# Edge counts of a graph network built in groups of 18 targets instead of 25, with packed group numbers and counts stored in pieces

## What is computed

```python
h = relu(layernorm(x)); x = x + relu(segment_sum((h @ W0)[src] * w[:, None], dst))          # layer 0
h = relu(layernorm(x)); deg, norm ...; x = x + relu(segment_sum(norm * (h @ W1.T + b)[row], col))  # layer 1, with self loops
h = relu(layernorm(x)); a = h + segment_sum(h[src], dst); x = x + relu(a @ G1 + g1) @ G2 + g2  # layer 2
h = relu(layernorm(x)); x = x + concat of 8 heads of softmax-weighted segment_sum(Wx[src], dst) # layer 3
```

## Time and profile before

| | |
|---|---|
| median of 3 executions | 2926.83 us (2922.68 to 2935.74) |
| the profiled execution's own time | 2952.38 us |
| its span, first to last instruction | 2951.1 us |
| mean granted TensorE clock | 0.933 |
| PE busy | 2508.8 us, 85% |
| DVE busy | 1854.8 us, 63% |
| ACT busy | 568.5 us, 19% |
| POOL busy | 872.3 us, 30% |
| build loop, first to last matmul | 801.6 to 1153.7 us |

### The profile page before, as it was taken

How to read it: one execution, slowest core, us unless ns; L and a number is a source line. 1 busy time by engine, 2 the same in 40 slices (tenths; PEclk the granted TensorE clock), 3 DMA queues, 4 the chain that set the end, 5 groups by cost and what they waited for, 6 DMA issues and landing times.

```text
span 2951.1 us, 39280 instructions
## 1 busy us (share of the span) xinstructions
PE 2508.8 (85%) x10397; PEld 1450.1 (49%) x10397; DVE 1854.8 (63%) x4953; ACT 568.5 (19%) x946; POOL 872.3 (30%) x900
## 2 busy tenths in 40 slices
PE   7888988877887777999989999997898588888777
PEld 5534443433444444666555555664787433333332
DVE  7765667586588885657333443334786387776666
ACT  4533310000055553000000000001555100000000
POOL 0366666666400000000000000000002466666665
PEclk9899999898888888999999999998999699999999
DMA  6686655666422112334711121112644466676665
GB/s 164 178 241 175 181 166 167 172 168 179 117 75 86 54 54 65 94 110 112 200 43 57 57 57 54 53 32 61 152 120 138 125 193 202 204 230 189 192 189 167
DMA packets 152926, 389.06 MB, mean 132 GB/s; under 512 B 40735, under 2 KB 42136, under 8 KB 152737
## 3 DMA queue, kind: packets, MB, share of 16 engines
q0 software_dynamic: 71040, 232.25, 27.6%
q1 hardware_dynamic: 81014, 153.03, 18.4%
q10 hardware_dynamic: 683, 1.28, 0.2%
HBM read 333.73 MB, written 52.72 MB: 131 GB/s over the span
## 4 chain that ended last, share of the span: by engine, by line
PE 53%; DVE 23%; issue 10%; DMA 7%; another core or an unknown queue 3%; POOL 2%; ACT 1%; SPq 1%; ACTq 0%; DVEq 0%
PE banks L1841 17%; PE banks L1979 15%; PE banks L1807 7%; DVE spare L1031 4%; PE banks L2156 4%; DVE spare L1030 3%; DMA ring<-edge_counts 3%; PE banks L1971 3%; DMA ring<-table,src_t 2%; POOL ring L2313 2%; DVE sel L1104 2%; PE banks L1796 1%; DVE ring L1583 1%; DVE rstd L884 1%
## 5 line engine op out<-in xcount | busy, mean ns | idle before, releaser
L1841 PE MATMUL banks<-ring,sel 128*125 128x512 f32 x1682 | 891.4, 658 | 160.5 <-issue 116.1
L1841 PEld LDWEIGHTS banks<-ring,sel 128*125 128x125 f32 x1682 | 287.0, 199 | 476.7 <-issue 473.4
L2258 POOL DMA_INDIRECT ring<-table,src_t x440 | 436.8, 993 | 250.5 <-issue 107.7
L2292 POOL DMA_INDIRECT x<-table,src_t x25 | 25.1, 1005 | 1493.1 <-DMA x<-src_digits 1478.4
L2313 POOL DMA_INDIRECT ring<-table,src_t x401 | 386.5, 964 | 227.9 <-PE banks L1845 98.4
L1979 PE MATMUL banks<-acc,ring 125*125 125x512 f16 x1900 | 437.9, 381 | 7.0 <-issue 7.0
L1971 PE MATMUL banks<-spare 128*125 128x325 f16 x1080 | 276.0, 370 | 73.2 <-DVE spare L1031 24.2
L1979 PEld LDWEIGHTS banks<-acc,ring 125*125 125x125 f16 x1900 | 256.9, 137 | 160.4 <-issue 27.2
L1583 DVE TENSOR_TENSOR ring<-ring,banks 128x512 f32<-128x512 f32 x388 | 255.7, 682 | 122.3 <-DMA ring<-table,src_t 99.2
L1971 PEld LDWEIGHTS banks<-spare 128*125 128x125 f16 x1080 | 152.2, 147 | 197.2 <-issue 194.7
L1031 DVE TENSOR_SCALAR spare<-node_scores,flags 128x650 f16<-128x650 f16 x540 | 207.7, 385 | 0.0
(11 more groups left out here) (408 smaller groups left out, 2970.9 us busy)
## 6 DMA issues: line engine op xcount, KB each, us to landing
ring<-edge_counts SPq DMA_DIRECT2D x38, 683.6 KB
edge_counts<-big SPq DMA_DIRECT2D x25, 683.6 KB
ring<-table,src_t POOLq DMA_INDIRECT x841
sel<-edge_counts SPq DMA_DIRECT2D x12, 683.6 KB
acc<-dst_places SPq DMA_DIRECT2D x28, 256.0 KB
x<-dst_places SPq DMA_DIRECT2D x27, 256.0 KB
acc<-src_digits SPq DMA_DIRECT2D x28, 224.0 KB
x<-src_digits SPq DMA_DIRECT2D x27, 224.0 KB
```

The source lines that it names most:

```text
L1841: last = P.matmul(to, sel[:, n % SELS, :], rows, start=False, stop=True, skip_group_check=True)
L2258: G.indirect_dma_start(out=ring[:, i % RING, :], out_offset=None, in_=table[0][:, :], in_offset=bass.IndirectOffsetOnAxis(ap=src_t[:, i:i ...
```

## The change

A group becomes 18 targets (the last one of a tile 17), 7 groups to a tile, 175 in all, so `BSTEPS` is 590. The key is 25 x 18 = 450 wide and fits one PSUM bank of 512: a step has one matmul instead of two, and four banks take turns (`MADE`) instead of two pairs. The group numbers of three steps are packed into one 32-bit word by DVE (`GROUP_PACK`, `GROUP_BITS`), so 20 registers last for 60 steps; PE shifts and masks. ACT loads the ends of four tiles' groups (28 registers) at once. The one-hot of the low number is made for five steps (`LB`) by one `tensor_tensor`, with a semaphore of its own (`low_ok`); the ring grows to 10. A tile of counts is stored, and the first four are loaded, in eight pieces of up to 16 rows, stores spread over the time of the next tile. ACT's border counts in layer 0 go from 124 to 174, and the tables of the groups grow with them.

```diff
-    GT = 5
-    GW_N = TN // GT
+    GT = 7
+    GW_N = -(-TN // GT)
+    GW_LAST = TN - (GT - 1) * GW_N
-    KEY_W = 2 * HALF_W
-    HOTS = 7
+    KEY_W = TILES * GW_N
+    HOTS = 10
+    GROUP_PACK, GROUP_BITS, GROUP_WORDS = 3, 8, 20
+    END_TILES = 4
+    MADE = 4
-    COUNTS_FIRST, COUNTS_EACH = 24, 10
+    COUNTS_FIRST, COUNTS_EACH = 34, 14
+    PIECES = -(-TN // 16)
...
-            return banks[:, 2 * n:2 * n + 2, 0:HALF_W]
+            return banks[:, n % MADE, 0:KEY_W]
...
+                if b == BRB - 1:
+                    own.mark(V.memset(group_row[:, BSTEPS:LISTED], float(GROUPS)))
+                    V.wait_ge(v_own, own.n)
+                    number = group_row.rearrange("p (w n) -> p w n", n=GROUP_PACK)
+                    for n in range(GROUP_PACK - 1, 0, -1):
+                        high = number[:, :, n] if n == GROUP_PACK - 1 else group_sum
+                        own.mark(V.tensor_scalar(out=group_sum, in0=high, scalar1=float(1 << GROUP_BITS), scalar2=None, op0=ALU.mult))
+                        V.wait_ge(v_own, own.n)
+                        own.mark(V.tensor_tensor(group_sum, group_sum, number[:, :, n - 1], ALU.add))
+                        V.wait_ge(v_own, own.n)
+                    own.mark(V.tensor_copy(group_words, group_sum))
+                    V.wait_ge(v_own, own.n)
...
                 if j >= HOTS:
                     V.wait_ge(built, j - HOTS + 1)
-                V.tensor_scalar(out=low_hot[j % HOTS], in0=low_names, scalar1=low_t[:, j:j + 1], scalar2=None, op0=ALU.is_equal).then_inc(hot_ok, 1)
+                if j % LB == 0:
+                    if j >= HOTS:
+                        V.wait_ge(built, j - HOTS + LB)
+                    V.tensor_tensor(low_room[:, j % HOTS:j % HOTS + LB, :], low_names[:, None, :].to_broadcast([128, LB, TN]),
+                                    low_t[:, j:j + LB, None].to_broadcast([128, LB, TN]), ALU.is_equal).then_inc(low_ok, 1)
                 V.tensor_scalar(out=key_hot[j % HOTS], in0=key_names, scalar1=key_t[:, j:j + 1], scalar2=None, op0=ALU.is_equal).then_inc(hot_ok, 1)
...
                     if q == 0:
-                        A.reg_load(end_regs[0:GT], group_end[0:1, n:n + GT])
+                        if t % END_TILES == 0:
+                            tiles_left = min(END_TILES, TILES - t) * GT
+                            A.reg_load(group_regs[0:tiles_left], group_end[0:1, n:n + tiles_left])
...
             for j in range(BSTEPS):
-                if j % LOADED_TILES == 0:
-                    P.reg_load(tile_regs, group_row[0:1, j:j + LOADED_TILES])
+                if j % GROUP_STEPS == 0:
+                    P.reg_load(tile_regs[0:GROUP_WORDS], group_words[0:1, j // GROUP_PACK:j // GROUP_PACK + GROUP_WORDS])
...
-                v = nc.s_assert_within(P.snap(tile_regs[j % LOADED_TILES]) & 127, 1, GROUPS,
+                word, at = P.snap(tile_regs[j // GROUP_PACK % GROUP_WORDS]), j % GROUP_PACK * GROUP_BITS
+                v = nc.s_assert_within((word >> at if at else word) & 255, 1, GROUPS,
-                P.wait_ge(hot_ok, 2 * (j + 1))
+                P.wait_ge(hot_ok, j + 1)
+                if j % LB == 0:
+                    P.wait_ge(low_ok, j // LB + 1)
                 P.wait_ge(room, v)
-                for h in range(2):
-                    to = banks[0:TN, bass.ds((v & 1) * 2 + h, 1), 0:HALF_W].rearrange("p a d -> p (a d)")
-                    last = P.matmul(to, low_hot[j % HOTS], key_hot[j % HOTS][:, h * HALF_W:(h + 1) * HALF_W],
-                                    start=False, stop=True, skip_group_check=True)
-                last.then_inc(built, 1)
+                to = banks[0:TN, bass.ds(v & (MADE - 1), 1), 0:KEY_W].rearrange("p a d -> p (a d)")
+                P.matmul(to, low_hot[j % HOTS], key_hot[j % HOTS], start=False, stop=True, skip_group_check=True).then_inc(built, 1)
...
-            def store_counts(t):
-                S.wait_ge(taken, GT * (t + 1))
+            def store_counts(t, piece):
+                S.wait_ge(taken, min(GROUPS, GT * (t + 1) + piece * GT // PIECES))
-                S.dma_start(counts_dram[t * TN:t * TN + TOP, :], rows[0:TOP]).then_inc(stored[(COUNTS_N + t) % 3], 16)
-                S.dma_start(counts_dram[t * TN + TOP:(t + 1) * TN, :], rows[TOP:TN]).then_inc(stored[(COUNTS_N + t) % 3], 16)
+                p0, p1 = 16 * piece, min(TN, 16 * piece + 16)
+                S.dma_start(counts_dram[t * TN + p0:t * TN + p1, :], rows[p0:p1]).then_inc(stored[(COUNTS_N + t) % 3], 16)
```

More of the change, by code:

```diff
@@ L251, in build @@
         acc16 = flat_acc.bitcast(F16).rearrange("p (t c) -> p t c", c=2 * D)
[L253 removed]
+        made16 = [big[:, n * MAKE_W:(n + 1) * MAKE_W].bitcast(F16)[:, 0:TILES * TN].rearrange("p (s r) -> p s r", r=TN) for n in range(MAKES)]
         slot16 = [flat_ring[:, n * SLOT_W:(n + 1) * SLOT_W].bitcast(F16)[:, 0:TILES * TN] for n in range(SLOTS - 1)]
@@ L258, in counts_at @@
             return slot16[n % SLOTS][0:TN, s * TN:(s + 1) * TN]
+        LB = 5
+        assert HOTS % LB == 0 and BSTEPS % LB == 0
         HOT_W = KEY_W // 2 + (TN + 1) // 2
-        key_hot = [flat_spare[:, n * HOT_W:n * HOT_W + KEY_W // 2].bitcast(F16) for n in range(HOTS)]
-        low_hot = [flat_spare[:, n * HOT_W + KEY_W // 2:(n + 1) * HOT_W].bitcast(F16)[:, 0:TN] for n in range(HOTS)]
+        key_hot = [flat_spare[:, n * KEY_W // 2:(n + 1) * KEY_W // 2].bitcast(F16) for n in range(HOTS)]
+        low_room = flat_spare[:, HOTS * KEY_W // 2:HOTS * KEY_W // 2 + HOTS * TN // 2].bitcast(F16).rearrange("p (n i) -> p n i", i=TN)
+        low_hot = [low_room[:, n, :] for n in range(HOTS)]
         assert HOTS * HOT_W <= 6 * D
@@ L489, in build @@
         keys_ok, keys_turned = signal("keys_ok"), signal("keys_turned")
-        hot_ok, built, room, taken = signal("hot_ok"), signal("built"), signal("room"), signal("taken")
+        hot_ok, low_ok, built, room, taken = signal("hot_ok"), signal("low_ok"), signal("built"), signal("room"), signal("taken")
         slot_in = [signal(f"slot_in{n}") for n in range(SLOTS)]
@@ L549, in place_value @@
         def place_value(k):
-            return 32 * len(range(k % NB, 2 * TILES, SLOTS)) + 16 * (k // NB + 1)
+            return slot_value(2 * TILES - SLOTS + (k - 2 * TILES) % SLOTS) + 16 * (k // NB + 1)
         TABLE_N, COUNTS_N, H2_N, LAST_N = (n * TILES for n in range(4))
         def wait_stored(engine, n):
-            engine.wait_ge(stored[n % 3], 32 * (n // 3 + 1))
+            engine.wait_ge(stored[n % 3], sum(16 * PIECES if COUNTS_N <= m < H2_N else 32 for m in range(n % 3, n + 1, 3)))
         def pair_step(n):
@@ L648, in vector_program @@
             own.mark(V.tensor_copy(gstep_f[:, :], gstep_i[:, :]))
-            V.tensor_scalar(out=group_bias, in0=node_iota[:, 0:GROUPS - 1], scalar1=-float(GW_N), scalar2=0.5 - GW_N, op0=ALU.mult,
-                            op1=ALU.add).then_inc(consts, 1)
+            starts = group_start.rearrange("p (t q) -> p t q", q=GT)
+            own.mark(V.tensor_scalar(out=starts, in0=node_iota[:, 0:TILES, None].to_broadcast([128, TILES, GT]), scalar1=-float(TN), scalar2=0.5,
+                                     op0=ALU.mult, op1=ALU.add))
+            V.wait_ge(v_own, own.n)
+            V.scalar_tensor_tensor(out=starts, in0=node_iota[:, None, 0:GT].to_broadcast([128, TILES, GT]), scalar=-float(GW_N), in1=starts,
+                                   op0=ALU.mult, op1=ALU.add).then_inc(consts, 1)
             def step_tables():
@@ L1648, in count_groups @@
                                  accum_out=group_counts[:, g:g + 1]).then_inc(group_counted, 1)
+            group_regs = [A.alloc_register(f"group_end{n}") for n in range(END_TILES * GT)]
             def take_groups():
@@ L1951, in tensor_program @@
             P.wait_ge(keys_ok, BRB + 1)
-            for pair in (1, 0):
-                P.matmul(bank[2 * pair][0:TN, 0:HALF_W], zeros, wide[:, 0:HALF_W], start=True, stop=True)
-                P.matmul(bank[2 * pair + 1][0:TN, 0:HALF_W], zeros, wide[:, 0:HALF_W], start=True, stop=True).then_inc(room, 1)
+            for v in range(1, MADE + 1):
+                P.matmul(bank[v % MADE][0:TN, 0:KEY_W], zeros, wide[:, 0:KEY_W], start=True, stop=True).then_inc(room, 1)
             for j in range(BSTEPS):
-                if j % LOADED_TILES == 0:
-                    P.reg_load(tile_regs, group_row[0:1, j:j + LOADED_TILES])
+                if j % GROUP_STEPS == 0:
+                    P.reg_load(tile_regs[0:GROUP_WORDS], group_words[0:1, j // GROUP_PACK:j // GROUP_PACK + GROUP_WORDS])
                 if j == 16:
@@ L2420, in sync_program @@
             for t in range(TILES):
-                store_counts(t)
-                if 3 <= t < 3 + SLOTS:
-                    load_counts(t - 3)
+                for piece in range(PIECES):
+                    store_counts(t, piece)
+                    if 4 <= t < 4 + SLOTS:
+                        first_counts(t - 4, piece)
```

56 lines of the change are left out of this document (31 added, 25 removed).

## The result

The changed kernel takes 2915.86 us against 2930.74 us for the kernel before (medians of 20 executions each): a ratio of 0.9946, interval 0.9934 to 0.9957, some 16 us less where 46.6 were forecast. One execution of the changed kernel, of 3904 us at a mean granted clock of 0.553, is left out of the ratio. The time lies at the very end of the stated range (2842 to 2916), which bears out nothing of the sum: the saving is a third of the forecast. The profiled execution took 2933.06 us, 19.3 less than that of the kernel before. Both were long ones, 17.2 and 21.6 us over these medians.

What follows compares the result with a forecast made beforehand. PE, through its sequencer, was taken to lead the build loop: 279.7 + 12.7 + 10.3 = 302.7 us against 352.1. With 2 (layer 0) and 0.8 (stores) added, 46.6 us less: 2880 us, range 2842 to 2916.

Steps and rivals of the forecast that it cites:

- The step of PE: Build loop: one matmul instead of two gives 0.412 us a step; shifts in two steps of three make it 0.474.
- The wait on `low_ok`: Build loop, every fifth step: one more PE instruction of 0.09 us, 40 to 118 times, up to 10 us, not added separately.
- the 10.3 us below: Rest of the old loop beyond its steps, kept in the new sum: mainly layer 0's tail and a few long loads.
- DVE's cover: Build loop: batch and first key need 1.05 us while PE has five ready steps, 2.4 us; so DVE's batch is covered.
- Fewer loads: Build loop: nine register loads at 1.41 us, 12.7 us instead of 37; a tenth stands ahead of the first step.
- Four banks: Build loop: ACT keeps up, PE may be four groups ahead; the 0.017 us a step of waits taken as gone.
- Layer 0: Ahead of the build loop: 2 us more for packing, bounds 0 and 12; larger tables cost no pace, border counts hidden.
- The tail: Behind the build loop: issuing the last tile's eight store pieces costs 0.8 us more, bounds 0 and 2.1.
- The free shift: Rival in the build loop: shift costs nothing, step 0.412 us, loop 266 us, 83 less in all, 2844 us; chance 0.14.
- the slow loads: Rival about loads, given as slower than the kernel before; chance 0.08. A register load over 3 us would count against the forecast.
- The third rival: Sequencer eats the gain: extraction and waits make steps 0.536 us, loop 339, 10 us less in all, 2917; chance 0.12.
- Its own signs: Trace checks: loop about 303 us, dense part 5 to 6 us behind the last step; wrong if loop starts over 10 late.

## Why the prediction was wrong, point by point

- **The step of PE, right.** 0.412 without a shift was forecast, 0.40 measured; 0.505 with one, 0.50 measured. The shift is one more ALU_OP (983 on that line, 590 + 393), 0.097 us start to start. Without the separate wait the loop takes 304.2 us; 302.7 was forecast.
- **The wait on `low_ok`, the first step that failed.** The prediction saw it, priced it at up to 10 us and left it "within the 10.3 us below". That rest was already spoken for: it came from the loop before, where no such wait exists, and 279.7 + 12.9 for steps and loads (9 x 1.434) with the 14.5 of the wait leave 319.2 - 307.1 = 12.1 us of it still there. A cost that is new must be a term of its own. It was also 0.11 us each in its own step, and 0.137 by the loop's time, not 0.09.
- **DVE's cover, right but for the start.** The batch took 0.811 us (0.805 forecast), the keys start 0.25 apart as forecast, and from step 60 on the batch costs nothing. In the first 60 steps, where DVE does layer 0's tail too, it costs 5 us, which explains part of the 12.1; the prediction argued the cover only for a DVE that has nothing else to do.
- **Fewer loads, right, and worth nothing.** Ten loads of 1.434 us at the median. But the prediction's own terms, set side by side, had 590 x 0.062 = 36.6 us for shifts against 20 x 1.41 = 28.2 us of loads saved; it took the packing as given and never compared.
- **Four banks, right.** PE waited 3.4 us for ACT; under 3 was forecast. ACT's loads took 2.41 us at the median, not 1.9, seven times, behind cover.
- **Layer 0, the second step that failed.** 2 us, bounds 0 to 12; some 16 measured. About half of it is the tables, which were in the bounds and put at 0 for a wrong reason: the earlier trace rows compare the stretch with the tables to the next one, which has its own delays, and not to the same stretch without them. That DVE was busy for 37.8 of 40 us there before the change says it better: it had no room. Four pairs more cost 7 us on the kernel before, and thinner table work gave back 10 in the changed one. The gather of the key rows was left out of the sum altogether: `BRS`, a fifth of `BSTEPS`, goes from 108 to 118, five gathers get ten rows more, and the prediction priced none of their issues. Its delay is shown (POOL's stop of 6.7 us, PE's wait of 9.9); how much of the 16 us it is isn't: 8 us added to the kernel before, but only 1.5 to 2 regained in the changed one. All four additions together cost the kernel before 23 us.
- **The tail**: 0.8 forecast, 1.4 measured, within its bounds.
- **The rivals.** The free shift and the slow loads didn't happen. The third rival named the time (2917), but by chance: it put 0.186 us, extraction and waits together, on two steps of three, which would have cut the loop by 13 us. The loop lost 33, and the rest of the time went into layer 0.
- **Its own signs** gave it away: the loop started 22.9 us late, where over 10 was to mean wrong, and the dense part started 7.2 us behind the last step, not 5 to 6.

## What to carry to other kernels

Price a new wait as an instruction of its own wherever the waiting engine's sequencer leads, and put its count into the sum; two producers that count up one semaphore in a fixed order need one wait. When a loop's trip count changes, follow it to every shape that is made from it, those of the transfers above all: 118 rows were gathered more slowly than 120. Work that is added to a stage whose engine has no idle time there can cost nearly its length (7 us of 8.3 here), and giving it out more thinly can take that back. Before a wait is put down to an engine, look whether that engine was done long before: the waits of the kernel without packing were register loads.

## What the runs showed of the hardware

- Five gathers of 118 rows of 1.5 KB took POOL 1.64 to 1.71 us each, stopped it for 6.7 us and left four tenths and fewer of the DMA engines busy; with 108 or 120 rows they took 0.98 to 1.21 us and stopped nothing.
- A wait instruction that stands alone on PE's sequencer shows 0.051 us in the trace, takes 0.106 from its start to that of the next instruction, and made its step 0.109 us longer.
- The loop's pace did not follow TensorE's clock: at a granted 0.78 in the mean (between the levels of 1.2 and 2.4 GHz) the kernel without packing kept steps of 0.40 us, while the one with single one-hots at 0.90 needed 0.50 for two steps of three, those with a shift. Steps with neither shift, wait nor load took 0.412 us in the mean at 0.90, and 0.419 in the changed kernel at 0.75. Rows of the first two for the loop:

```profile
790.00:1086.70 296.70, 240.83 (x606) 95.44 (x605) 252.29 (x1183) 187.97 (x345) 0.00 (x0) 0.78 0.26 75
```
```profile
810.40:1109.30 298.90, 244.81 (x606) 86.99 (x605) 276.75 (x1183) 188.15 (x345) 0.00 (x0) 0.90 0.46 74
```
